# A two-layer graph kernel: the relation table first, the edge plan made between its batches, the norm's wide operations on GpSimd

## What is computed

```python
h = relu(layernorm(x))                       # layer 0
msg = sum over r of (h[src] where type == r) @ weight[r]
x = x + segment_sum(msg, dst)
h = relu(layernorm(x))                       # layer 1
mean = segment_sum(h[src], dst) / max(count(dst), 1)
out = mean @ W_l + b_l + h @ W_r
out = out + zeros.at[dst].set(edge_attr @ W_e + b_e)
x = x + out
```

## Time and profile before

| what | time |
|---|---|
| median of 3 runs | 4608.56 us (4601.85 to 4614.72) |
| profiled execution, its own time | 4609.9 us |
| profiled execution, span of the core | 4608.1 us |

### The profile page before, as it was taken

One profiled execution on the slowest core, in us unless ns is written; L12 is line 12 of the kernel. 1 busy time (PEld: TensorE's weight loads), 2 busy tenths in 40 slices (PEclk: granted clock), 3 DMA queues, 4 the chain that ended last, 5 costly groups with the idle time before them and its releaser, 6 DMA issues.

```text
span 4608.1 us, 83210 instructions
## 1 busy us (share of the span) xinstructions
PE 3015.5 (65%) x23324; PEld 2428.0 (53%) x23325; DVE 3502.2 (76%) x17508; ACT 2067.4 (45%) x6530; POOL 3113.6 (68%) x3190
## 2 busy tenths in 40 slices
PE   1464555555565666666666776776767777777799
PEld 1123444444444554455455555655656666666699
DVE  5564778778787877787878888787888878888823
ACT  0242445545455554544545545444554544545400
POOL 1017777777777777777777777777777777777700
PEclk9985667777777777787788888888888989998999
DMA  9882333333323433243342343423333333333289
GB/s 101 255 312 60 103 103 118 114 110 110 104 84 100 141 121 112 70 134 92 100 141 88 107 122 98 123 82 113 108 93 112 113 94 106 102 86 86 71 328 381
DMA packets 315345, 575.60 MB, mean 125 GB/s; under 512 B 124155, under 2 KB 227259, under 8 KB 303515
## 3 DMA queue, kind: packets, MB, share of 16 engines
q1 hardware_dynamic: 135494, 443.69, 26.8%
q0 software_dynamic: 101568, 105.81, 11.4%
q10 hardware_dynamic: 77842, 20.86, 3.7%
HBM read 334.10 MB, written 248.81 MB: 126 GB/s over the span
## 4 chain that ended last, share of the span: by engine, by line
POOL 53%; issue 17%; PE 15%; DMA 9%; DVE 3%; ACTq 1%; another core or an unknown queue 1%; ACT 0%; POOLq 0%; DVEq 0%; SPq 0%
POOL msg L723 52%; DMA msg<-rel_table,arena 8%; PE ps L485 6%; PE ps L1148 4%; PE ps L1048 2%; PE ps L1132 1%; POOL wrel L714 1%; ACTq L852 1%; PE ps L1074 1%; DVE onehot L1252 1%; DMA arena<-in_dst 0%; DMA arena<-counts 0%; DVE batch L1392 0%; DVE arena L670 0%
## 5 line engine op out<-in xcount | busy, mean ns | idle before, releaser
L723 POOL DMA_INDIRECT msg<-rel_table,arena x3125 | 3049.9, 976 | 953.7 <-issue 917.8
L890 ACT CAST arena<-ps 128x392 bf16<-128x392 f32 x3136 | 1327.5, 510 | 2014.8 <-PE ps L1074 2008.0
L485 PE MATMUL ps<-onehot,msg 128*81 128x128 f32 x6250 | 1081.9, 335 | 1121.1 <-DMA msg<-rel_table,arena 1065.1
L485 PEld LDWEIGHTS ps<-onehot,msg 128*81 128x81 f32 x6250 | 920.1, 191 | 1231.0 <-DMA msg<-rel_table,arena 1081.0
L1392 DVE TENSOR_SCALAR batch<-iota_h,wrel 128x196 bf16<-128x196 bf16 x4312 | 1248.4, 294 | 0.0
L1391 DVE TENSOR_SCALAR batch<-iota_h,wrel 128x128 bf16<-128x128 bf16 x4312 | 1174.6, 275 | 1.3 <-PE ps L1074 1.3
L503 DVE TENSOR_SCALAR onehot<-iota_w,arena 128x128 f32<-128x128 f32 x3125 | 685.4, 299 | 583.5 <-PE ps L485 577.1
L1074 PE MATMUL ps<-batch 128*128 128x196 bf16 x4312 | 764.9, 288 | 185.1 <-DVE batch L1392 87.5
L900 ACT ACTIVATE msg<-attr,arena 128x16 f32<-128x16 f32 x3125 | 679.6, 315 | 70.9 <-PE ps L485 57.1
L1132 PE MATMUL ps<-arena 128*128 128x192 bf16 x7238 | 690.2, 254 | 0.0
L1132 PEld LDWEIGHTS ps<-arena 128*128 128x128 bf16 x7238 | 637.1, 102 | 7.0 <-issue 0.3
(11 more groups left out here) (148 smaller groups left out, 1116.0 us busy)
## 6 DMA issues: line engine op xcount, KB each, us to landing
arena<-counts SPq DMA_DIRECT2D x458, 224.0 KB, 4.5
rel_table<-arena SPq DMA_DIRECT2D x98, 512.0 KB, 3.4
msg<-rel_table,arena POOLq DMA_INDIRECT x3125
counts<-arena SPq DMA_DIRECT2D x10, 3136.0 KB
arena<-counts SPq DMA_DIRECT2D x28, 896.0 KB, 12.1
attr<-in_edge_attr SPq DMA_DIRECT2D x125, 200.0 KB
counts<-arena SPq DMA_DIRECT2D x8, 2688.0 KB
arena<-counts SPq DMA_DIRECT2D x31, 672.0 KB, 10.6
```

Of the source, the lines that this page charges most:

```text
L485: mm = pe.matmul(ps[0:rows, bank, 0:WIN], msg[:, k, 0:rows], onehot[:, k, :], start=(k == 0), stop=(k == K - 1))
L723: pool.indirect_dma_start(msg[:, k, 0:D], None, table0, bass.IndirectOffsetOnAxis(ap=idx[:, c // NG, k:k + 1].bitcast(U32), axis=0)).then_ ...
L890: nc.scalar.copy(cblk[:, h, :, u * WU * WD:(u + 1) * WU * WD].rearrange("p t (w d) -> p w t d", d=WD), unit_cols(b, u).rearrange("p w (t d ...
```

## The change

The table comes first. x is loaded with 98 consecutive nodes in each partition (long rows), so a tile now holds nodes that lie 98 apart, and the tile's store writes 128 rows of 4 KB at a distance of 392 KB. x is loaded again during the main stage, in seven pieces, in the old layout.

dst, src and types are loaded with one superblock per partition (125 partitions x 3200 edges, and 112 more for dst and src). Each of these loads is divided at 112 partitions, a multiple of 16, with the rest in a second transfer. The plan's steps work on those rows, one step per table batch (`plan_step`). The results that the main stage needs with 128 edges of a superblock across the partitions (`idx`, `last`, `rel`) are turned by PE in 21 groups of four small transposes (`turn_edges`), and ACT copies them out (`take_turn`). Seven histogram steps come ahead of the table, three in each of batches 0 to 10.

Of the norm, GpSimd does the subtraction, the square and the wide product; DVE keeps the two sums and the reciprocal. ACT copies the tiles 1, 3 and 5 of a batch whole, DVE the right halves of the others. The loops over table batches are written out.

The packed edges are stored by SP behind batch 3. The table of runs is made in the main stage, by SP, in 16 parts of 1600 rows at slots 0, 10, 40, 70, and so on; GpSimd's gather of runs waits for the parts that it needs. The core of the diff:

```diff
         @block.gpsimd
...
-            pool.wait_ge(s_idx, 16)
-            pool.wait_ge(s_typ, 16)
-            pool.wait_ge(s_pack, 2)
-            nc.gpsimd.tensor_single_scalar(idx, idx, R, ALU.mult).then_inc(s_rowno, 1)
-            pool.wait_ge(s_rowno, 1)
-            nc.gpsimd.tensor_tensor(idx, idx, typ_i, ALU.add).then_inc(s_rowno, 1)
...
+            def center(n):
+                h = n % 2
+                pool.wait_ge(FA["neg"], n + 1)
+                if n >= 2:
+                    pool.wait_ge(FA["norm"], n - 1)
+                    pool.wait_ge(FA["var"], n - 1)
+                nc.gpsimd.tensor_tensor(cen[:, h], tiles(x_sb, n), spread(stat[:, h, 0, :]), ALU.add).then_inc(FA["cen"], 1)
+                pool.wait_ge(FA["cen"], n + 1)
+                nc.gpsimd.tensor_tensor(sqr[:, h], cen[:, h], cen[:, h], ALU.mult).then_inc(FA["sq"], 1)
+
+            def normal(n):
...
+            center(0)
+            center(1)
+            normal(0)
+            normal(1)
+            for n in range(NB - 2):
+                center(n + 2)
+                normal(n + 2)
+
+            pool.wait_ge(s_turned, len(turns))
+            pool.wait_ge(s_plan, 1)
             for b in range(TB):
                 pool.wait_ge(tstored[b], 16 * NB)
...
         @block.sync
...
+            sp.wait_ge(s_xfill, 1)
+            for p0, p1 in ((0, P - 16), (P - 16, P - 1)):
+                sp.dma_start(x_flat[p0:p1], x[p0 * NT:p1 * NT].rearrange("(p t) d -> p (t d)", t=NT)).then_inc(s_x, 16)
...
+            for n in range(NB):
+                store_rows(n, n % 2)
+                if n == 3:
+                    sp.wait_ge(s_pack, 2)
...
+            def store_runs(j):
+                r0, r1 = j * RUN_ROWS, min((j + 1) * RUN_ROWS, MAXRUN)
...
+                sp.dma_start(runs[r0:r1, :],
+                             bass.AP(ends.tensor, ends.offset + r0 * GRAIN, [[GRAIN, r1 - r0], [1, P]])).then_inc(s_runs, 16)
...
                     if c % NG == 1 and c // NG + 1 < S:
                         load_attr(c // NG + 1, c // NG + 1)
+                    if c >= 0 and c in run_store_at:
+                        store_runs(run_store_at.index(c))
+                    if c % NG == 3 and 0 <= c // NG < X_PARTS:
+                        load_x(sp, c // NG)
...
         @block.scalar
...
-            act.dma_start(edges(ends), packed).then_inc(s_ends_out, 16)
-            act.wait_ge(s_ends_out, 16)
-            act.dma_start(runs[0:MAXRUN, :],
-                          bass.AP(ends.tensor, ends.offset, [[GRAIN, MAXRUN], [1, P]])).then_inc(s_runs, 16)
...
             def take_rows(m, q, n, h):
+                take_turn(n, 0)
                 for t in range(TB):
...
+                        if t in ACT_ROWS:
+                            nc.scalar.copy(tbuf[:, t], ps[:, bank:bank + 2, :]).then_inc(FA["actout"], 1)
+                        else:
+                            nc.scalar.copy(tbuf[:, t, 0], ps[:, bank, :]).then_inc(FA["actout"], 1)
+                    if t == 2:
+                        take_turn(n, 1)
+                    if t == 5:
+                        take_turn(n, 2)
+                    if t == 5 and n + 2 < NB:
+                        deviation(act, FA, n + 2, h)
...
         @block.tensor
...
             def table_batch(n, h):
+                plan_step(n)
                 pe.wait_ge(FA["norm"], n + 1)
...
                 mm.then_inc(FA["hT"], 1)
...
+                turn_edges(n, 0)
+                if n >= 1:
+                    rel_rows(n - 1, 1 - h, n)
+                for c in range(HIST_FIRST + n * HIST_EACH, min(HIST_FIRST + (n + 1) * HIST_EACH, FR // HC)):
+                    hist_step(c)
...
         @block.vector
...
+                if n == 3:
+                    link(nc.vector.tensor_tensor(last_n, after, here, ALU.is_lt))
+                if n == 4:
+                    link(nc.vector.tensor_reduce(bad[0:S, 1:2], last_n, AX, ALU.max))
+                if n == 5:
+                    link(nc.vector.tensor_reduce(col[0:S, 0:1], here, AX, ALU.min))
...
+            for c in range(HIST_FIRST):
+                hist_onehots(c)
+            dve.wait_ge(s_x, 48)
...
                 for t in range(TB):
+                    if t == 0 and n == 8:
+                        plan_step(n)
+                    if t == 0 and n + 2 < NB:
+                        row_sums(n + 2)
+                    if m >= 0 and t not in ACT_ROWS:
                         dve.wait_ge(FA["rows"], m * TB + (t + 1))
...
                         nc.vector.tensor_copy(tbuf[:, t, 1],
                                               ps[:, 5 + 2 * ((q + t) % 2), :]).then_inc(FA["dveout"], 1)
...
+                    if n < NB:
+                        if t in (0, 1, 2):
+                            hist_onehots(c + t)
+                        if t == 3 and n != 8:
+                            plan_step(n)
+                        if t == 2 and n + 2 < NB:
+                            square_sums(n + 2)
+                        if t == 5 and n + 2 < NB:
+                            inverse(n + 2)
```

More of the change, by code:

```diff
@@ L336, in gnn_two_layers @@
         NORM = ["sum", "cen", "sq", "var", "std", "rstd", "norm"]
-        FA = family("table", NORM + ["hT", "relu", "rows", "actout", "dveout"])
+        FA = family("table", NORM + ["neg", "hT", "relu", "rows", "actout", "dveout"])
         FB = family("mid", NORM + ["cols", "sumT", "x1", "cnt", "inv", "h", "hT", "back", "sign", "bias", "base",
@@ L364, in edges, with dve_rows, x_tiles, load_x @@
             return v.rearrange("(s p k) -> p s k", p=P, k=K)
+        def dve_rows(i):
+            return i // TB * (TB - len(ACT_ROWS)) + sum(t not in ACT_ROWS for t in range(i % TB))
+        def x_tiles(j):
+            return j * (NT // X_PARTS), min((j + 1) * (NT // X_PARTS), FULL)
+        def load_x(sp, j):
+            t0, t1 = x_tiles(j)
+            sp.dma_start(x_sb[:, t0:t1], xv[:, t0:t1]).then_inc(s_x2, 16)
+            if t1 == FULL:
+                sp.dma_start(x_sb[0:PART, FULL], x[FULL * P:N, :]).then_inc(s_x2, 16)
         def n_from(n, least):
@@ L823, in _ @@
             with sp.Else():
+                for j in range(X_PARTS):
+                    load_x(sp, j)
                 for_steps(sp, load_attr)
@@ L1003, in _, with hist_step @@
         def _(pe):
-            def hist_step(c, q, first=False, end=False):
+            def hist_step(c):
                 pe.wait_ge(s_hoh, c + 1)
                 for k in range(HC):
-                    mm = pe.matmul(ps[:, 7, 0:NP], hoh[:, q, k, 0:P], hoh[:, q, k, P:P + NP],
-                                   start=(k == 0 and first), stop=(k == HC - 1 and end))
+                    mm = pe.matmul(ps[:, 2, 0:NP], hoh[:, c % HOHS, k, 0:P], hoh[:, c % HOHS, k, P:P + NP],
+                                   start=(k == 0 and c == 0), stop=(k == HC - 1 and c == FR // HC - 1))
@@ L1010, in hist_step @@
                 mm.then_inc(s_hmm, 1)
-            HS = FR // HC
-            hist_step(0, 0, first=True)
-            hist_step(1, 1)
-            with pe.Fori(1, HS // 2 - 1) as i:
-                for q in range(2):
-                    hist_step(i * 2 + q, q)
-            hist_step(HS - 2, 0)
-            hist_step(HS - 1, 1, end=True)
-            pe.wait_ge(s_hist, 1)
-            pe.matmul(ps[0:NP, 6, 0:P], hist[:, :], ones[:, :], start=True, stop=True).then_inc(s_tot, 1)
-            pe.wait_ge(s_totc, 1)
@@ new lines, in turn_edges @@
+            def turn_edges(n, j):
+                if (n, j) not in turn_at_point:
+                    return
+                i = turn_at_point[n, j]
+                v, k0, k1 = turns[i]
+                pe.wait_ge(s_edges, v + 1)
+                if i >= 1:
+                    pe.wait_ge(s_turned, i)
+                if i == ROWS_AFTER:
+                    pe.wait_ge(s_rowsc, 1)
+                pe.nop(nofuse=True)
+                for k in range(k0, k1):
+                    mm = pe.transpose(ps[:, 3, (k - k0) * S:(k - k0 + 1) * S], by_edge[v][:, k, :], ident[0:S, 0:S])
+                mm.then_inc(s_turn, 1)
```

405 lines of the change are left out of this document (245 added, 160 removed).

## The result

The changed kernel takes 4524.4 us (median of four runs, 4521.5 to 4535.9) where the kernel before, run beside it, took 4605.2 us: a ratio of 0.9839 with a 95% interval of 0.9813 to 0.9864. The prediction was 4515 us, between 4462 and 4562 us. Single executions of one kernel lie up to 35 us apart here, so the moment of the first gather, which the profile gives, is the sharper measure of everything that happens ahead of it.

The account below looks back on a forecast made before the run. Time was taken as first gather, a 4064 us stage paced by GpSimd's gathers, and a tail: 4609.9 - 97 (earlier first gather) + 3 (contention) = 4516 us, 4515 us against the median; range 4462 to 4562 us.

Parts of the forecast that it names:

- The start: Everything ahead of the first row copy: expected near 36 us, 150 us earlier than before, bounds 30 and 48 us.
- dst's landing: In the opening loads: dst, sharing the engines with as much of x, lands near 14 us.
- Batches 1 to 7: Table batches that carry plan steps: 103.6 us together, 112 us with PE's part stretched.
- the chain that was predicted: Per early batch: DVE's copies, histogram and plan step through copy 4, 9.4 us, then PE's part, 4.1 us, plus any turning.
- the stretch of PE by its clock: In batches 1 to 7: PE's part a quarter longer at a lower granted clock, 1.2 us a batch, 8 us.
- step 7: Plan step with two passes: 6.2 us if the second runs as the shift, 7.8 us if as L1285; 7 taken.
- Batches 8 to 14: Later table batches, without a long plan step and paced by PE: 71.7 us, last copy at 220 us.
- The main stage: Gathers after the table: contention from 28 MB more adds 0 to 6 us, 3 us taken; no wait for runs.
- The stores never paced the early batches: Denies rival 1: plan hidden, stores pace the table at 1.33 us per tile, 4461 us; chance 0.12.
- stay at 1.2 GHz: Rival 2, first case: PE at the lower clock through the table, batches some 16.5 us, 4562 us; chance 0.14 with the lock.
- the lock: Rival 2, second case: GpSimd locks DVE out, up to 3.3 us in 12 batches, 4555 us; chance 0.14 with the clock.
- The third rival: Main stage: pieces of runs and x slow each gather, not faster from 31 ns more; chance 0.07.

Follow-up runs that it names:

- dst alone: Changed kernel with x loaded only after dst has landed, src and types only after x: 4522.3 us, ratio 0.982 to the kernel before.
- ACT's copies: Changed kernel with ACT making all seven row copies whole in the first seven batches: 4496.2 us, ratio 0.975 to the kernel before.

## Why the prediction was right, point by point

**The gain's place and the sum.** It came from the first gather, 78.7 us earlier where 97 us were predicted, and 4.7 us were given back in the main stage where 3 us were. Against the profiled run of before that makes 4535.9 us (4516 predicted). Against the medians it is 80.8 us of gain, 93.6 predicted.

**The start is the term that was mis-sized.** 36 us were predicted for the first row copy, with 48 us as the upper bound; it came at 55.5 us. 15.5 of the 19.5 us are dst's landing, 29.5 us in place of 14 us. Two figures of that step failed. Loads were put at the 399 GB/s of the stores and moved 230 GB/s. And dst was to share the engines with as much of x, 3.2 MB in all, where 5.75 MB had begun by 29.5 us: the whole of x, ahead of dst for the most part, and some of src. By an estimate from these numbers the rate is the smaller part: 3.2 MB take 13.9 us at 230 GB/s and 8.0 us at 399 GB/s, so some 6 of the 15.5 us are the rate and the rest is what moved beside dst. dst alone landed at 13.4 us. Why x's queue got the larger share is not shown. The last 4 us lie between the histogram's first seven steps (8.5 us with the preparation, as predicted) and the copy. Of them 3 us are the next three steps, which PE's queue puts ahead of the second transposes and which GpSimd's wide products stretch to 6.22 us. Moving the three operations to DVE does not win them back (first copy 55.2 us), since DVE then has the operations themselves.

**Batches 1 to 7** took 112.8 us where 112 us were predicted, by the chain that was predicted: copies behind the plan step, then PE's tile, histogram, transposes and tile. That the sum is met to 0.8 us is luck in part: one by one, from copy 0 to copy 0, the batches lie between 1.0 us below and 1.5 us above their forecasts (with the 1.2 us for the clock). ACT's copies, which cut the chain, shorten the batches by a quarter; a plan step moved within the same list shortens DVE's wait for PE and pays as much elsewhere. Of the sum's parts the stretch of PE by its clock, put at 8 us, measured 9.2 us at the first gather when PE was kept busy. The second pass of step 7 ran as the shift (1.89 us, the lower of the two bounds).

**Batches 8 to 14**, from copy 0 of batch 7 to the last copy, took 67.3 us for the 71.7 us predicted: 10.5 to 11.2 us each where the sum had 11 to 11.5 us while turnings stood there. From the last copy to the first gather it was 8.6 us, not 6: the last store lands 5.6 us after its issue, near the last one of before and not the median of the earlier trace rows. So 19.5 + 0.8 - 4.4 + 2.6 us are the some 18 us by which the first gather was missed.

**The main stage** is within what can be told: from the first gather to the end, the kernels without added transfers spread over 4274 to 4294 us. The bytes grew by 15.1 MB (499.3 MB from 325 us on before, 514.4 MB from 250 us on after), which at 0.2 us per MB would be 3 us; the scatter is larger, so that 3 us were predicted is neither confirmed nor refuted. The gathers' mean is 977 ns, and they waited 0.3 us in all for the runs.

**The rivals.** The stores never paced the early batches (share 0.61). PE did not stay at 1.2 GHz throughout: it was there behind a pause (0.50 in the stretch above), and that part is in the sum. Nor did the lock cost 40 us more: it is not in the sum, and 5.5 us of it are seen on the histogram. The third rival needed 31 ns more per gather; it was 1 ns.

## What to carry to other kernels

When a long step is slid into an engine's in-order list, look at who waits for the instructions behind it: here moving the step along the list brought other waits, and taking the awaited copies to another engine won 33.5 us, for a few lines. Price a start by the rate of loads in the direction and shape in question, not by that of stores, and by all the bytes queued beside the first load, and load first the few columns that the first batch needs. A pause that one engine left on PE was paid a second time in PE's clock; idle products in it brought the first gather 9.2 us forward, which the whole time does not show.

## What was not expected of the hardware

- Loads into SBUF with rows of 12.8 to 25 KB filled the DMA engines (share 0.99 to 1.03) at 230 GB/s on two queues and 267 GB/s alone; stores of 4 KB rows reached 399 GB/s at the same share.
- Two queues that loaded at once did not share evenly: by 21 us x (rows of 25 KB) had 3.16 MB under way and dst (rows of 13 KB) 1.29 MB.
- Loads of 124 and 125 rows kept about 4 of the 16 engines busy (0.27), and small loads of another queue came late beside them (first tile at 82.3 us).
- While GpSimd computes, a scaling of seven numbers per partition on DVE (L1388) took up to 1.26 us; alone it takes 0.17 us.
